# GpSimd waits for two free ring slots at every second chunk instead of one at each chunk, in a graph attention layer

## What is computed

```python
Q_h = (x @ Wq + bq).reshape(N, H, D)          # N = 12500, H = 8 heads, D = 12
K_h = (x @ Wk + bk).reshape(N, H, D)
V_h = (x @ Wv + bv).reshape(N, H, D)
E = (edge_attr @ We + be).reshape(-1, H, D)   # 412500 edges
score = K_h[src_idx] * Q_h[dst_idx] / sqrt(D) * E
score = exp(clip(score.sum(-1, keepdims=True), -5.0, 5.0))
msg = V_h[src_idx] * score
wV = segment_sum(msg, dst_idx, num_segments=N)
Z = segment_sum(score, dst_idx, num_segments=N)
return layernorm(x + (wV / (Z + 1e-06)).reshape(N, H * D))
```

## Time and profile before

| | |
|---|---|
| median of 3 runs | 5340.88 us (5330.81 to 5349.86) |
| the profiled execution | 5341.94 us |
| its span, first to last instruction | 5340.3 us |
| TensorE busy | 3563.3 us, 67% |
| GpSimd busy | 3143.5 us, 59% |
| VectorE busy | 2090.0 us, 39% |
| ScalarE busy | 1722.8 us, 32% |
| share of the 16 DMA engines, most of the span | 0.4 |

### The profile page before, as it was taken

The page is one execution under the profiler, slowest core; times in us unless marked ns, Lnnn a source line. Parts: engine busy times, 40 slices in busy tenths (PEclk is TensorE's granted clock), DMA queues, the critical chain, the costliest instruction groups (busy, mean ns, idle before and its releaser), DMA issues.

```text
span 5340.3 us, 72730 instructions
## 1 busy us (share of the span) xinstructions
PE 3563.3 (67%) x19972; PEld 3422.0 (64%) x19973; DVE 2090.0 (39%) x5996; ACT 1722.8 (32%) x3602; POOL 3143.5 (59%) x3249
## 2 busy tenths in 40 slices
PE   7666666666666666666666666666666666666664
PEld 6666666666666666666666666666666666666663
DVE  4333334333333333333333433333334333433346
ACT  4332333323332332333233332333333232323337
POOL 4556656665666656656665666566566665666560
PEclk7555555555555555555555555555555555555555
DMA  7444444444444444444444444444444444444442
GB/s 227 107 109 110 119 109 109 111 118 109 109 111 117 110 108 111 116 111 109 111 116 112 109 112 113 113 109 111 110 118 109 110 115 113 109 110 116 112 109 84
DMA packets 497768, 607.49 MB, mean 114 GB/s; under 512 B 256053, under 2 KB 420224, under 8 KB 497630
## 3 DMA queue, kind: packets, MB, share of 16 engines
q0 software_dynamic: 155200, 318.39, 22.5%
q1 hardware_dynamic: 233215, 281.36, 18.0%
q10 hardware_dynamic: 109330, 7.48, 1.5%
HBM read 584.51 MB, written 22.46 MB: 114 GB/s over the span
## 4 chain that ended last, share of the span: by engine, by line
PE 51%; issue 27%; another core or an unknown queue 13%; DVE 4%; ACT 2%; DVEq 1%; DMA 0%; ACTq 0%; POOL 0%; SPq 0%; POOLq 0%
PE bank L633 18%; PE bank L647 17%; PE bank L631 11%; PE bank L640 5%; DVE kqe L915 2%; DVE raw_score L926 1%; DVEq L303 1%; ACT spare L814 0%; DVE oh L910 0%; ACT spare L802 0%; ACT accP L792 0%; PE bank L597 0%; ACT eaT L760 0%; DVE kqe L907 0%
## 5 line engine op out<-in xcount | busy, mean ns | idle before, releaser
L530 POOL DMA_INDIRECT kv<-kv_table,src_idx x3224 | 3118.9, 967 | 2059.6 <-DVE msg L919 1020.4
L633 PE MATMUL bank<-w_e,eaT 97*128 97x96 f32 x6448 | 1886.1, 391 | 282.1 <-issue 282.1
L631 PE MATMUL bank<-ident,ea 128*96 128x128 f32 x3224 | 1354.9, 421 | 920.4 <-issue 610.5
L633 PEld LDWEIGHTS bank<-w_e,eaT 97*128 97x128 f32 x6448 | 1778.6, 333 | 290.4 <-issue 288.8
L907 DVE TENSOR_TENSOR kqe<-kv,bank 128x384 f32<-128x384 f32 x806 | 446.4, 554 | 3157.5 <-remote 2428.7
L631 PEld LDWEIGHTS bank<-ident,ea 128*96 128x96 f32 x3224 | 806.2, 250 | 928.7 <-issue 594.5
L647 PE MATMUL bank<-oh,msg 128*104 128x32 f32 x6448 | 1276.8, 355 | 172.3 <-issue 170.0
L647 PEld LDWEIGHTS bank<-oh,msg 128*104 128x104 f32 x6448 | 1225.4, 290 | 168.7 <-issue 166.0
L757 ACT ACTIVATE msg<-score 128x32 f32<-128x32 f32 x806 | 184.8, 229 | 3504.8 <-remote 2565.3
L640 PEld LDWEIGHTS bank<-q_win,ohT 96*128 96x128 bf16 x3224 | 398.3, 154 | 414.5 <-issue 408.2
L640 PE MATMUL bank<-q_win,ohT 96*128 96x96 bf16 x3224 | 448.5, 279 | 299.6 <-issue 295.5
(11 more groups left out here) (81 smaller groups left out, 525.8 us busy)
## 6 DMA issues: line engine op xcount, KB each, us to landing
ea<-in_edge_attr_dram SPq DMA_DIRECT2D x201, 768.0 KB
dst_b<-dst_by_chunk SPq DMA_DIRECT2D x201, 384.0 KB
kv<-kv_table,src_idx POOLq DMA_INDIRECT x3224
q_win<-q_table SPq DMA_DIRECT2D x806, 19.9 KB
kv_table<-kv_out SPq DMA_DIRECT2D x25, 336.0 KB
q_table<-q_out SPq DMA_DIRECT2D x25, 252.0 KB
spare<-in_x_dram SPq DMA_DIRECT2D x25, 168.0 KB
out_dram<-spare SPq DMA_DIRECT2D x25, 168.0 KB
```

The lines of the kernel that those rows point to most:

```text
L530: pool.indirect_dma_start(kv[:, slot, g, :], None, kv_dram[:, :], bass.IndirectOffsetOnAxis(ap=src_idx[:, u, g:g + 1], axis=0)).then_inc(k ...
L631: last = nc.tensor.transpose(eaT_ps[u % 2][0:D, g * P:(g + 1) * P], ea[:, u, g, :], ident[:, :])
L633: nc.tensor.matmul(e_ps[v % 2][:, g * D:(g + 1) * D], eaT[:, v % 2, g * P:(g + 1) * P], w_e[:, :], start=True, stop=True)
```

## The change

`step` on GpSimd waits for free slots only where u is even, and asks there for one message more, so that the slots of two chunks are free at once. The eight gathers of the two chunks then follow each other with no wait for a slot between them. `slots_taken` is added to once in two chunks. No other engine's program is touched; the number, shape and target of the gathers are the same.

```diff
             def step(s, u, _):
                 slot = u % RING
-                at_least(pool, msg_ready, s - RING + 1)
+
+                if u % 2 == 0:
+                    at_least(pool, msg_ready, s - RING + 2)
                 if u % IDX_GROUP == 0:
...
-                pool.sem_inc(slots_taken, 1)
+                if u % 2 == 0:
+                    pool.sem_inc(slots_taken, 1)
                 for g in range(G):
                     pool.indirect_dma_start(kv[:, slot, g, :], None, kv_dram[:, :],
```

## The result

The changed kernel takes **5384.47 us** (median of 5 runs, 5380.04 to 5405.45), the kernel before beside it 5349.86 us (median of 5, 5330.81 to 5353.93): a ratio of 1.0083, 95% interval 1.0055 to 1.0111. That is slower, by more than the 0.3% that the prediction took as the limit. The forecast was "no change" and 5345 us; the time lies inside the range, near its upper end.

The account below looks back on a forecast made before the run. The prediction took TensorE, slowed while GpSimd issues gathers, as the bound. Steady state -2, start +1 and end +2 gave +1 us on 5341.94 us; taken as +4 in all, 5345 us, range 5300 to 5392.

Parts of the forecast that it names:

- What bounds the kernel: Edge loop: TensorE's steps are slowed while GpSimd issues gathers, 6.4 us a chunk against 4.05 without gathers.
- a speed of 0.54 beside gathers: TensorE in the loop: constant speed of 0.54 while gathers are issued, giving about 6.35 us a chunk whatever the order.
- a period that differs although the burst is unbroken: Loop check: a difference over 0.1 us would mean the speed beside gathers is not constant and the sum is wrong.
- The removed and dropped instructions at zero: GpSimd at odd chunks: removed wait, register operation and count hide behind the 0.30 us between gathers, zero.
- The form of the burst: GpSimd in the loop: 16 unbroken gathers of about 20 us from an even chunk, then one 5 to 6 us pause.
- Rival A: GpSimd in the loop: bursts break after eight gathers, slower, likely 5390 us, 5830 if all break; chance 0.20.
- C: VectorE in the loop: waits for the delayed even chunk's gather to land, up to +790 us, 6130 us; chance 0.02.
- B: TensorE in the loop: gains more from one long rest of GpSimd than from two, 5291 us; chance 0.15.
- The steady state: Whole loop: 198 periods of 25.44 us in place of 25.45, -2 us, bounds -24 and +8.
- the 1.12 us in the earlier trace: GpSimd's idle time ahead of 2522.35 once in a period: does not go away, moves to the burst's end.
- The start: First wait for a slot: ends one step later, costing between 0 and +4 us, taken as +1.
- The end: Last burst: 16 gathers in place of 12, ending 5 us later, +2.3 us, bounds 0 and +5.

Follow-up runs that it names:

- e8: Kernel before with only two of each chunk's four gathers from chunk 8 on; 3490.21 us.
- e10: Changed kernel with each gather from chunk 8 on fetching rows of 384 bytes in place of 768; 5366.28 us.
- e16: Changed kernel with a 0.67 us pause of GpSimd behind every third gather; 5047.91 us, ratio 0.9441 to the kernel before.
- e12: Changed kernel with a 0.67 us pause of GpSimd behind every second gather; 5482.61 us.
- e3: Changed kernel with the pairs begun at odd chunks in place of even ones; 5796.74 us.
- e5: Kernel before with only the stronger demand at even chunks, odd chunks' waits and all counts kept; 5383.78 us, ratio 1.0040 to the kernel before.
- e2: Changed kernel, unchanged, measured and profiled again; 5373.16 us, ratio 1.0031 to the kernel before.
- e17: Kernel before with a 0.67 us pause of GpSimd behind every third gather; 5080.64 us, ratio 0.9495 to the kernel before.
- e18: Repeat of e16, timed closely beside e17; 5053.53 us, ratio 0.9449 to the kernel before.
- e6: Changed kernel with a 2.2 us pause of GpSimd in a burst's first chunk, once in 16 chunks; 5465.23 us, ratio 1.0191 to the kernel before.
- e14: Changed kernel with a 0.09 us memset behind every gather, its end waited for only ahead of the next memset; 5829.22 us, ratio 1.0903 to the kernel before.

## Why the prediction was wrong

**What bounds the kernel: half right.** That TensorE is held up while GpSimd issues, and is not limited by its clock or by full DMA engines, stands (e8, e10, e16). That it has a speed of 0.54 beside gathers does not: with half the gathers the speed is 1 (e8), and with rows of two or three TensorE no longer sets the pace (e12, e16). The prediction said what would show this, a period that differs although the burst is unbroken; e3 shows it most plainly, 27.7 us against 25.5.

On that point the prediction had spoken against the Trainium skill ("SBUF — State Buffer", section "Who interferes with whom"). By that rule DMA traffic doesn't get in TensorE's way. Here e10 agrees as far as bytes go: half of them changed nothing. What e8 and e16 show is a hold-up by the way gathers are issued, which a rule on memory ports does not foresee. Whether a memory port has a part in it no run shows.

**The removed and dropped instructions at zero: right**, within the 0.1% by which e5 and e2 differ; and priced by e17 and e18 for the case that the cover goes.

**The form of the burst: right.** 16 gathers, one pause of 5.1 to 5.6 us, from an even chunk, 25.46 us without a late gather. Rival A (bursts of eight) did not occur but for one burst in 200, and C (a late landing) and B did not either.

**The steady state, "198 x (25.44 - 25.45) = -2 us": this is the step that failed**, with +6 to +25 us measured, bounds -24 and +8. The step took the period of the unbroken burst as the same wherever a burst starts, and so put a stop at a burst's start at nothing; the runs show 18 late gathers there, at 1.1 us a period some 19 us. The price of the period was read from stretches of nine and sixteen periods whose bursts mostly begin one chunk later (3 mod 4) than those of the change: the two late gathers in them, at chunks 138 and 446, stand in the last chunk of a burst, where they cost nothing. The row that would have warned was within reach: three bursts of the kernel before that begin with chunk 50, 578 or 600 have a period of 26.4 to 26.5 us, and 13 gaps of 1.70 us, mostly 44 chunks or a multiple of that apart, stand out among 0.30s. The prediction treated the 1.12 us in the earlier trace rows as time that just moves to the burst's end, and rightly: it is itself a wait for a message, and ends 2.52 us after the product at 2519.83, as the long pause ends 2.50 us after the one at 2529.40. But it did not ask what else lies in the first chunk of the new burst, and there a microsecond isn't free (e6).

**The start, +1: not far off.** The first wait for a slot ends 7.4 us after the first product now, 5.1 before, +2.3 us. Around it the scatter of the first product, 128 to 155 us over all profiles, is larger. **The end, +2.3**: the last burst has 16 gathers as forecast, and from the last gather to the last product it is 20.2 us in both kernels; a share of its own can't be told.

**The measured 0.8%** is thus the sum of a real cost in the loop (6 to 25 us, or 0.1% to 0.5%), and of scatter ahead of it and in the old loop's rhythm, which fell in favour of the kernel before in that comparison. e2 with 0.3% and e5 with 0.4% rest on more executions.

**That 5384 us lies inside the range is luck.** The forecast's own bounds were 5318 and 5359. The range went up to 5392 for the sake of rival A at 5390, and A did not occur.

**What stays open**: what the late gather is and why it needs a stop ahead of it, why the loop of the kernel before varies by 20 us, why e14's memset holds a step back, and by which path rows of gathers hold up TensorE. That a slot, a queue or a semaphore is shared was not tried apart.

## What to carry to other kernels

In a closed loop a wait has no price by itself; find the event that restarts the waiting engine, and ask of every moved microsecond whether it comes before that event (it counts in full) or after (it vanishes in the pause). Before summing a slowdown as a speed, change the density of what causes it: here 0.67 us of silence after every third gather gained 5.5%, more than any rearrangement of the waits. A small cost that hides in a gap comes back only where the engine is the bound and the gap is taken up by something else. And a price read from a regular stretch holds for that phase of the loop: look what stands at the place to which the change moves the start of a burst.

## What the hardware showed unexpectedly

TensorE's records and its signals come apart during a burst. In the kernel after, the sums L650 of three steps follow each other at TensorE's own pace, and the fourth comes 13.3 us later (start us, duration us):

```profile
1893.05 1.56 PE L650 MATMUL bank<-oh,msg 128*104 128x32 f32 x8
...
1897.10 1.56 PE L650 MATMUL bank<-oh,msg 128*104 128x32 f32 x8
...
1901.15 1.56 PE L650 MATMUL bank<-oh,msg 128*104 128x32 f32 x8
...
1914.47 1.56 PE L650 MATMUL bank<-oh,msg 128*104 128x32 f32 x8
```

VectorE, which starts a product when the step's signal arrives, sees something else:

```profile
1889.01 0.55 DVE L910 TENSOR_TENSOR kqe<-kv,bank 128x384 f32<-128x384 f32 x1 [9.05 <-remote]
1891.39 0.55 DVE L910 TENSOR_TENSOR kqe<-kv,bank 128x384 f32<-128x384 f32 x1
1894.64 0.55 DVE L910 TENSOR_TENSOR kqe<-kv,bank 128x384 f32<-128x384 f32 x1 [0.73 <-PE bank L650]
1903.63 0.56 DVE L910 TENSOR_TENSOR kqe<-kv,bank 128x384 f32<-128x384 f32 x1 [6.62 <-PE bank L650]
1914.35 0.55 DVE L910 TENSOR_TENSOR kqe<-kv,bank 128x384 f32<-128x384 f32 x1 [8.35 <-remote]
```

The step that ends at 1893.05 + 1.56 = 1894.61 is seen at once (1894.64). The next two end at 1898.66 and 1902.71 by TensorE's records and are seen at 1903.63 and 1914.35, 5.0 and 11.6 us later; the trace's own record of `pe_step` has it rise at 1903.61 and 1914.33. Either the signals are held back while a long row of gathers is issued, or the recorded starts run ahead of the work; the trace doesn't tell which. In e8, where TensorE isn't held up, all but a few of the 770 recorded signals follow their step's recorded end within 0.02 us.
